# Depthwise 3x3 taps on TensorE: from two 128x128 matmuls per tap to four 64x64 matmuls per tap, the lower half image read from a copy with exchanged channel halves

## What is computed

```python
def _L0_conv_ref(x, ...):
    h = lax.conv_general_dilated(x, dw_w, (1, 1), ((1, 1), (1, 1)), feature_group_count=C_IN)   # depthwise 3x3
    h = jax.nn.relu(_bn(h + dw_b, ...))
    h = _prune(h, 4.0)                       # a channel with amax below 4.0 becomes zero
    h = conv_1x1(h, pw_w) + pw_b             # pointwise
    return _prune(jax.nn.relu(_bn(h, ...)), 0.001)

x = x + _L0_conv_ref(_ln_c(x))               # layer norm over channels first
t = _to_tokens(x)
t = t + _L0_ffn_ref(_ln_t(t), ...)           # 8 experts, each takes its 1024 best tokens
return _from_tokens(t, x)
```

## Time and profile before

| | us |
|---|---|
| three runs | 503.77, 503.83, 505.05 |
| median | 503.83 |
| span of the profiled execution | 502.9 |
| around the span (lowest run less span) | 0.9 |
| PE busy, whole span | 361.9 (72%) |
| DVE busy, whole span | 327.1 (65%) |
| ACT busy, whole span | 274.3 (55%) |

### The profile page before, as it was taken

The page is one execution under the profiler, slowest core; times in us unless marked ns, Lnnn a source line. Parts: engine busy times, 40 slices in busy tenths (PEclk is TensorE's granted clock), DMA queues, the critical chain, the costliest instruction groups (busy, mean ns, idle before and its releaser), DMA issues. The chain is left out here.

```text
span 502.9 us, 6936 instructions
## 1 busy us (share of the span) xinstructions
PE 361.9 (72%) x1947; PEld 255.7 (51%) x1947; DVE 327.1 (65%) x1004; ACT 274.3 (55%) x587; POOL 159.3 (32%) x151
## 2 busy tenths in 40 slices
PE   4989888888889985631021798999990498876575
PEld 3656555566666553520011374677560467464453
DVE  5699988888889898578879548556620025235444
ACT  3577888888888876677640528556551240510000
POOL 4000000000000000000005777787888788876000
PEclk9999999999999997655555799999997598997755
DMA  4604555555554342479101223344443267847998
GB/s 103 188 38 141 185 168 185 167 185 168 185 182 150 130 131 96 137 238 392 71 1 33 55 56 94 95 65 64 83 85 34 55 189 134 194 61 169 285 390 344
DMA packets 36396, 72.01 MB, mean 143 GB/s; under 512 B 6385, under 2 KB 16785, under 8 KB 36369
## 3 DMA queue, kind: packets, MB, share of 16 engines
q1 hardware_dynamic: 24256, 56.52, 35.0%
q0 software_dynamic: 9472, 8.66, 11.2%
q10 hardware_dynamic: 2640, 6.51, 3.3%
HBM read 34.96 MB, written 30.29 MB: 130 GB/s over the span
## 5 line engine op out<-in xcount | busy, mean ns | idle before, releaser
L403 POOL DMA_INDIRECT picked<-token_rows,slot_idx x32 | 31.5, 986 | 270.7 <-issue 270.4
L691 PE MATMUL psC<-x_pad,tap_diag 128*128 128x392 f32 x256 | 90.8, 498 | 6.7 <-ACT x_pad L570 5.6
L1009 DVE SCALAR_TENSOR_TENSOR conv<-x_pad,taps_w,conv 128x784 f32<-128x784 f32 x64 | 65.9, 1030 | 0.8
L691 PEld LDWEIGHTS psC<-x_pad,tap_diag 128*128 128x128 f32 x256 | 46.1, 189 | 37.0 <-DVE conv L1009 5.1
L1302 DVE TENSOR_TENSOR y_sum<-psC,b_rows 128x512 f32<-128x512 f32 x15 | 10.4, 692 | 75.2 <-PE psC L869 75.2
L869 PE MATMUL psC<-w,hid 128*128 128x128 f32 x480 | 56.6, 280 | 2.2 <-ACT hid L633 2.1
L869 PEld LDWEIGHTS psC<-w,hid 128*128 128x128 f32 x480 | 55.8, 197 | 4.6 <-issue 3.0
L613 ACT ACTIVATE picked_T<-psA 128x512 f32<-128x512 f32 x16 | 9.0, 594 | 59.9 <-PE psA L836 59.9
L426 POOL DMA_INDIRECT moe_sum_late<-y_rows,slot_idx x24 | 37.9, 1581 | 9.5 <-issue 7.0
L483 ACT ACTIVATE rows<-psD,sm 112x128 f32<-112x128 f32 x98 | 35.7, 464 | 9.3 <-DVE sm L1001 9.3
L729 PE MATMUL psB<-act,pw_masked 128*128 128x392 f32 x64 | 27.9, 563 | 17.0 <-DVE pw_masked L1085 17.0
(11 more groups left out here) (211 smaller groups left out, 728.8 us busy)
## 6 DMA issues: line engine op xcount, KB each, us to landing
token_rows<-rows SPq DMA_DIRECT2D x16, 416.5 KB, 3.6
x_in<-in_x_dram SPq DMA_DIRECT2D x16, 392.0 KB, 3.5
x_res<-in_x_dram SPq DMA_DIRECT2D x16, 392.0 KB, 4.3
moe_sum<-zero_rows SPq DMA_DIRECT2D x16, 392.0 KB, 4.9
x_all<-x SPq DMA_DIRECT2D x16, 392.0 KB, 2.9
moe_sum_late<-zero_rows SPq DMA_DIRECT2D x16, 392.0 KB, 7.7
out_dram<-act ACTq DMA_DIRECT2D x16, 392.0 KB, 6.2
w<-in_L_ffn_W_dram SPq DMA_DIRECT2D x16, 256.0 KB, 3.3
```

What stands on the lines that cost most here:

```text
L403: nc.gpsimd.indirect_dma_start(out=picked_in[k][:, b, :], out_offset=None, in_=rows_dram, in_offset=bass.IndirectOffsetOnAxis(ap=slot_idx[ ...
L691: ins = nc.tensor.matmul(psC[:, h, 0:HALF].rearrange("c (h w) -> c h w", w=W), tap_diag[:, n, :], x_pad_v[:, q, y0:y0 + LINES, dx:dx + W], ...
L1009: return nc.vector.scalar_tensor_tensor(o, x_pad_v[:, q, y0 + dy:y0 + dy + lines, dx:dx + W], taps_w[:, PE_TAPS + n:PE_TAPS + n + 1], acc, ...
```

## The change

The change to the taps on PE:

1. Each tap of a half image, one matmul with a diagonal 128x128 matrix, becomes two matmuls with 64x64 matrices: channels 0 to 63 and 64 to 127 apart. The four matmuls of one tap of the whole image use the four quarters of the 128x128 array: the upper half image from `x_pad` (rows 0-63 to columns 0-63, rows 64-127 to columns 64-127) and the lower half image from a copy, `x_turned`, in which the channel halves are exchanged (rows 0-63 to columns 64-127, rows 64-127 to columns 0-63). All of this is `conv_taps`.
2. The copy is two DMAs of 64 partitions x 480 elements per image, at the front of SP's step, behind a wait for `x_pad`. It lies in `hid`, and so does `zero_rows` now.
3. `conv_taps` does the whole image at one place of PE's step, where the lower half was; nothing stands where the upper half was. It waits for the copy too (s_xtu), and raises s_conv once.
4. On DVE both `first_tap` calls stand at the end of the step, behind the residual sum and the moments.
5. The setup loads the tap weights twice more with exchanged halves (two DMAs), and writes eight diagonals of 64 columns in place of four of 128, and a half identity.
6. Before the experts ACT waits for all zero stores to `moe_sum_late`, since they read from `hid`.

`PE_TAPS` is 4 in both kernels, so five taps stay on DVE.

```diff
+HC = C // 2
+LOWER = (LINES + 2) * PW
...
-        zero_rows = sb("zero_rows", [P, TPI * C])
...
-        tap_diag = sb("tap_diag", [128, PE_TAPS, 128])
+        taps_turned = sb("taps_turned", [128, 9])
+        ident_half = sb("ident_half", [128, HC])
+        tap_diag = sb("tap_diag", [128, PE_TAPS, HC])
+        tap_turned = sb("tap_turned", [128, PE_TAPS, HC])
...
+        zero_rows = hid[0:P, 0, 0:TPI * C]
+        x_turned = hid[:, 1:3, 0:LOWER]
+        x_turned_v = x_turned.rearrange("c q (h w) -> c q h w", w=PW)
...
+            sp.dma_start(taps_turned[0:HC, :], taps_d[HC:C, :]).then_inc(s_prm, 16)
+            sp.dma_start(taps_turned[HC:C, :], taps_d[0:HC, :]).then_inc(s_prm, 16)
             load_x(1, 1)
 
             def step(pair, u):
+                on, img, q, use = image(pair, u, 1)
+                if on:
+                    sp.wait_ge(s_pad, img * 2 + 2)
+                    for to, of in ((0, HC), (HC, 0)):
+                        sp.dma_start(x_turned[to:to + HC, q, :], x_pad[of:of + HC, q, LINES * PW:LINES * PW + LOWER])\
+                            .then_inc(s_xtu[q], 16)
                 on, img, q, use = image(pair, u, -2)
...
-                        act.wait_ge(s_conv, img * 2 - 2)
+                        act.wait_ge(s_conv, img - 1)
...
+            act.wait_ge(s_lz, 16 * B)
             for e in range(E):
                 expert(e)
...
-            def conv_half(img, q, h):
+            def conv_taps(img, q, use):
+                pe.wait_ge(s_pad, img * 2 + 2)
+                pe.wait_ge(s_xtu[q], use * 32 + 32)
                 if since(img, 1):
-                    pe.wait_ge(s_taken, img * 2 + h - 1)
+                    pe.wait_ge(s_taken, img * 2)
+                pe.sem_inc(s_pe, 1)
                 for n in range(PE_TAPS):
                     dy, dx = TAPS[n]
-                    y0 = h * LINES + dy
-                    ins = nc.tensor.matmul(psC[:, h, 0:HALF].rearrange("c (h w) -> c h w", w=W), tap_diag[:, n, :],
-                                           x_pad_v[:, q, y0:y0 + LINES, dx:dx + W],
-                                           start=(n == 0), stop=(n == PE_TAPS - 1))
+                    for half, weights, lines in ((0, tap_diag, x_pad_v), (1, tap_turned, x_turned_v)):
+                        for row in range(2):
+                            of = slice(row * HC, row * HC + HC)
+                            col = row if half == 0 else 1 - row
+                            ins = nc.tensor.matmul(psC[col * HC:col * HC + HC, half, 0:HALF].rearrange("c (h w) -> c h w", w=W),
+                                                   weights[of, n, :], lines[of, q, dy:dy + LINES, dx:dx + W],
+                                                   start=(n == 0), stop=(n == PE_TAPS - 1))
                 ins.then_inc(s_conv, 1)
...
-                if on1:
-                    if isinstance(img1, int) and img1 == 0:
-                        pe.wait_ge(s_setup, 1)
-                    pe.wait_ge(s_pad, img1 * 2 + 1)
-                    conv_half(img1, q1, 0)
...
                 if on1:
-                    pe.wait_ge(s_pad, img1 * 2 + 2)
-                    conv_half(img1, q1, 1)
+                    if isinstance(img1, int) and img1 == 0:
+                        pe.wait_ge(s_setup, 1)
+                    conv_taps(img1, q1, use1)
...
-                dve.wait_ge(s_prm, 16 * 11)
+                dve.wait_ge(s_prm, 16 * 13)
...
+                nc.vector.tensor_tensor(ident_half[:, :], ident[:, 0:HC], ident[:, HC:C], ALU.add).then_inc(s_tiny, 1)
+                dve.wait_ge(s_tiny, 5)
                 for n in range(PE_TAPS):
-                    nc.vector.tensor_scalar(tap_diag[:, n, :], ident[:, :], taps_w[:, n:n + 1], None, ALU.mult)
+                    nc.vector.tensor_scalar(tap_diag[:, n, :], ident_half[:, :], taps_w[:, n:n + 1], None, ALU.mult)
+                    nc.vector.tensor_scalar(tap_turned[:, n, :], ident_half[:, :], taps_turned[:, n:n + 1], None, ALU.mult)
...
-                if on1:
-                    first_tap(img1, q1, 0)
-                    if onN:
-                        moments_b(img0 + 1, new)
+                if on1 and onN:
+                    moments_b(img0 + 1, new)
...
-                if on1:
-                    first_tap(img1, q1, 1)
                 if on4 and not onN:
                     moments_b(img0 + 1, new)
                     moments_c(img0 + 1, new)
+                if on1:
+                    first_tap(img1, q1, 0)
+                    first_tap(img1, q1, 1)
```

More of the change, by code:

```diff
@@ L246, in build @@
         s_x1c = pair_of("x1_kept")
+        s_xtu = pair_of("lower_half_turned")
         s_t3, s_m3, s_std3, s_n3, s_rl = (sem(n) for n in (
@@ L270, in build @@
         s_bits, s_nest, s_fit, s_end = (sem(n) for n in ("next_bits", "nested_ready", "fitting_ready", "search_end"))
-        s_pool, s_act = sem("pool_past_waits"), sem("act_past_waits")
+        s_pool, s_act, s_pe = sem("pool_past_waits"), sem("act_past_waits"), sem("pe_past_waits")
         ctx.enter_context(nc.allow_low_precision(reason="a partition's counts are whole numbers up to HW: fp16 holds them exactly"))
@@ L288, in _ @@
                 sp.dma_start(prm[:, n:n + 1], src.rearrange("(c a) -> c a", a=1)).then_inc(s_prm, 16)
-            sp.dma_start(taps_w[:, :], dw_w.rearrange("c a h w -> c (a h w)")).then_inc(s_prm, 16)
+            taps_d = dw_w.rearrange("c a h w -> c (a h w)")
+            sp.dma_start(taps_w[:, :], taps_d).then_inc(s_prm, 16)
+            sp.dma_start(taps_turned[0:HC, :], taps_d[HC:C, :]).then_inc(s_prm, 16)
+            sp.dma_start(taps_turned[HC:C, :], taps_d[0:HC, :]).then_inc(s_prm, 16)
             load_x(1, 1)
             def step(pair, u):
+                on, img, q, use = image(pair, u, 1)
[4 more added lines that the diff above has]
+                            .then_inc(s_xtu[q], 16)
                 on, img, q, use = image(pair, u, -2)
@@ L304, in step @@
                     sp.dma_start(y_t[:, ds(img, 1), :, :].rearrange("p i t c -> p (i t) c"),
-                                 zero_rows[:, :].rearrange("p (t c) -> p t c", c=C)).then_inc(s_yz, 16)
+                                 zero_rows.rearrange("p (t c) -> p t c", c=C)).then_inc(s_yz, 16)
                 on, img, q, use = image(pair, u, 5)
@@ L329, in _ @@
                 sp.dma_start(late_t[:, ds(img, 1), :, :].rearrange("p i t c -> p (i t) c"),
-                             zero_rows[:, :].rearrange("p (t c) -> p t c", c=C)).then_inc(s_lz, 16)
+                             zero_rows.rearrange("p (t c) -> p t c", c=C)).then_inc(s_lz, 16)
             for e in range(2, E):
@@ L380, in _ @@
             nc.gpsimd.memset(x_pad[:, :, :], 0.0)
-            nc.gpsimd.memset(zero_rows[:, :], 0.0)
+            nc.gpsimd.memset(zero_rows, 0.0)
             nc.gpsimd.iota(tile_row[:, :], pattern=[[1, TPI], [TPI, B]], base=0, channel_multiplier=0,
@@ L1012, in first_tap @@
             def first_tap(img, q, h):
-                dve.wait_ge(s_conv, img * 2 + h + 1)
+                dve.wait_ge(s_conv, img + 1)
                 if since(img, 2):
@@ L1053, in setup_rest @@
                 nc.vector.tensor_scalar(part_i[:, 2:3], part_i[:, 0:1], 4, None, ALU.logical_shift_right).then_inc(s_tiny, 1)
-                dve.wait_ge(s_tiny, 6)
+                dve.wait_ge(s_tiny, 7)
                 nc.vector.scalar_tensor_tensor(tile_col[:, :], part_i[:, 1:2], float(TPI), part_i[:, 2:3], ALU.mult, ALU.add)\
                     .then_inc(s_tiny, 1)
-                dve.wait_ge(s_tiny, 7)
+                dve.wait_ge(s_tiny, 8)
                 nc.vector.tensor_scalar(before[:, :], tile_row[:, :], tile_col[:, :], None, ALU.is_gt)
```

## The result

| | before | after |
|---|---|---|
| runs, us | 503.77, 503.83, 505.03, 505.05 | 530.95, 534.91, 541.86, 543.74 |
| median, us | 504.43 | 538.38 |
| ratio | | 1.0554, 95% interval 1.0497 to 1.061 |
| span of the profiled execution, us | 502.9 | 540.0 (its time is 541.86) |
| mean granted clock of PE in it | 0.857 | 0.793 |

The change is slower by 5.5%, about 28 us. This ratio takes only the two shorter runs of the changed kernel (clock 0.81); with the two longer ones (clock 0.79), one of which is the profiled execution, the medians are 34 us apart. I had forecast 551 in 504 to 562. The direction was right and the size lies in the range, but the mechanism was not mine: the block of small matmuls ran as short as rival 1 said, and the time went to TensorE's clock, which I had not looked at as something the change could move.

A forecast was written before the change was run, and what follows sets the result against it. The prediction took a ring through ACT's row norm and DVE (11.91 us per step) as the bound, overtaken by the ring through the taps; 502.9 span + 0.9 + 35.6 steady steps + 12.1 fill = 551 us, range 504 to 562.

The forecast's parts named there:

- rival 1: All four array quarters run at once: block 3.18 us, steps still near 11.9 us, 508.2 us in all; chance 0.24.
- The upper-half taps cost nothing today.: PE's taps before the pointwise matmuls end at 110.32, and PE would wait for DVE's mask until 111.32 anyway.
- ring 1: Loop of row norm, PE's transposes and logits, DVE's statistics and on to the next norm; sets today's 11.91 us step.
- The block, 17 slots: The 16 small matmuls on PE take 17 slots of 0.33 us, 5.6 us, or 6.14 with both ends.
- Going in and out, 0.54: Array runs empty where tile size changes, at the block's two ends: 0.54 us per step, bounds nothing and 0.80.
- Ring 2: Loop from row norm through lower-half taps, x_pad copy and DVE's inverse; 11.28 us, predicted to become 14.78 and the bound.
- +35.6 for the steady steps: The 12 steps from image 3 to image 15 go from 140.8 us to 176.4 us.
- Fill, +12.1: Start of the convolution stage up to image 3's x_pad copy: 49.6 us instead of 37.49, 1.4 of it setup.
- 10.8: Time each for images 1 and 2 in the fill, us: copy 3.15, block 6.14 and 1.47; otherwise the prediction is wrong.
- DVE's move, 0.1 per step: Moving DVE's first tap uncovers a wait, about 0.1 us per step in ring 1; nothing if that no longer bounds.
- The copy hidden in steady steps: SP's exchanged-halves copy takes 3.15 us, but in steady steps the taps are 7.2 us away, so it costs nothing.
- the experts' wait free: ACT's new wait for zero stores before the experts has cover of over 30 us and costs nothing.

The follow-up runs named there:

- e4: Kernel before with one tap instead of four on TensorE for the upper half image, order and waits as before; 521.43 us, ratio 1.0309.
- e6: Changed kernel with all four taps of one array quarter issued before those of the next quarter; one run, 601.27 us.
- e11: Changed kernel with six taps on PE, later_tap 3 and 4 gone, plus the six filling matmuls of e5; 530.59 us, ratio 1.0495.
- e5: Changed kernel with six throwaway matmuls where the upper-half taps were, waiting only for the copy into x_pad; 514.55 us, ratio 1.0174.
- e9: e5 without the two copy DMAs per image and the waits for them, lower half computed from a constant; 511.39 us, ratio 1.0121.
- e2: Changed kernel without the two copy DMAs per image and the waits for them, lower half computed from a constant; 528.32 us, ratio 1.0433.
- e1: Changed kernel with five throwaway matmuls where the upper-half taps were, waiting for DVE's first taps; 520.14 us, ratio 1.0235.
- e3: Kernel before with full matmuls, both halves' taps in the lower half's place, first taps moved as in the change, no copy; 582.1 us, ratio 1.1531.

## Why the prediction was right, and where it was not

That the number came out in the range is luck. The forecast's own range was 542 to 562; it was widened down to 504 only to take in rival 1 at 508, and 538 lies between the two. A block sized at twice its length (6.14 us against 2.80) stood in for a fallen clock that the sum did not have.

- **"The upper-half taps cost nothing today."** True, and the step that failed all the same. I asked who waits for them, found nobody, and took them as free to remove. They were the cover of the clock. The 1.00 us hole of the earlier trace rows becomes 4.02 us, the clock falls in each step, and ring 1 grows by 1.75 us. The row that could have warned me is the earlier trace rows: the clock is not always full, it falls to 7, 6 and then 5 tenths at the end of this stage. The prediction quotes its 9s and does not treat them as something that the change can lose; no term of the sum and no rival has the clock in it. The Trainium skill, "TensorE: Matmul & The Clock Gate", section "HAM oscillation — how this bites in real kernels", describes a kernel that loses the clock in each iteration because PE waits for data in each; e4 shows a fall in each step here, where PE waits 2.8 to 3.0 us for DVE's mask. I had not applied it.
- **The block, 17 slots.** Measured 2.80 us, and 32 records in 8 slots. My reason, that records start in the order of the program, is refuted by the trace of the changed kernel (the second records of four matmuls start after the first records of all four) and by e6. The same page's section "Part 3: Packing small matmuls — row/col tiling" says that matmuls start and end strictly in program order; for these fp32 pairs the measurement decides against it: in e6 the fifth matmul starts at 83.61, ahead of the fourth, whose first record stands at 84.26. Rival 1 had the mechanism.
- **Going in and out, 0.54.** 2.80 less 8 x 0.33 leaves 0.16, near the lower bound. If the array is emptied, it costs no more than the 0.17 by which a last record outlasts its slot anyway.
- **Ring 2 becomes the bound, 14.78 us.** It did not: with 2.80 it is 11.44, and DVE's inverse at 122.32 waits for nothing. The ring itself was sound, as e11 shows within 0.2 us. The +35.6 for the steady steps against +32.1 measured is chance: two different sums, and 17.7 of the 32.1 are in the first four steps.
- **Fill, +12.1.** Measured +6.2. The setup (+1.4, 15.2 us) and the copy (3.15) came out at 15.3 and 3.1. The block of image 1 was less than half as long as forecast (2.79 against 6.14), that of image 0 4.39, part of it at half clock. Images 1 and 2 are 7.3 us apart in `x_pad` and not 10.8, which the prediction had named as a sign that it is wrong.
- **DVE's move, 0.1 per step.** About 0.16 in ring 1, and full-clock steps of 12.1 in e5 against the 11.9 of the earlier trace rows.
- **The copy hidden in steady steps, the experts' wait free.** PE waits for the copy twice in all, 4.9 us, both in the fill. Nothing of the loss is behind the convolution stage beyond 1 us: 36.0 of the 37.1 us of span are there at the last norm of rows.
- **Rival 1, 508 us.** Its block (3.18, measured 2.80) and its ring are what e5 shows, with a fill of +4.6 against its +3.2, and 514.55 us. Its main miss is the clock. Had I seen the block right, I would have said 508 and been off by 24 us by the ratio, 30 by the median.

In sum, as ratios: block, place, DVE order and setup 1.2% (e9), copy 0.5% (e5 less e9), clock 3.8% (changed kernel less e5). With the falling clock the copy comes out at 1.2% (changed kernel less e2), which these intervals do not tell from 0.5. The parts are differences of ratios, part of them from different chips, with intervals of about 0.4 to 0.6% each way, and e5's filling is counted as free, so they are good to about 0.7 of a per cent.

## What to carry to other kernels

Before taking work off TensorE because nobody waits for it, look at what the engine will do in its place: where a hole opens in each step (2.8 to 3.0 us were enough here), the work behind it may run at 1.2 GHz, and be on the path that sets the pace. Test it the cheap way: take the work out and leave all else alone, and put throwaway matmuls into the hole. And place several small matmuls on different quarters in turn, never one quarter after the other.

## What the hardware showed that I had not expected

- Less work made the kernel slower: three of four upper taps removed, nothing else, +3.1% (e4). More work made the changed kernel faster: six throwaway matmuls per step, 5.5% over the kernel before down to 1.7% (e5).
- Two step lengths in one run of one program, with the same hole of 1.7 us: steps of 12.1 to 12.4 while the clock held, 13.6 once it had fallen (e1). What decides between them is not shown.
- The clock can stay at the lower level for 10 us while PE is busy all the time (e3, 127.8 to 138.0).
- Four 64x64 fp32 matmuls on four quarters run as fast as one full one, the second record of each behind the first of all (2.80 us for 16). Issued one quarter after the other, the same 16 take 6.90 us.
